# Three moves in a fused decoder kernel: the gates' sums behind the first adapter round, GpSimd's sums released by the third norm's low parts, and the rank-4 product in wide instructions

## The reference

```python
x = x + attn(layernorm(x))            # scores q k^T, scaled; banded by sigmoid(score); softmax; values; projection
x = x + xattn(layernorm(x), ctx, ctx) # 8 heads; gates i, f from [q, k, v]; csum = cumsum(log_sigmoid(f)) along tokens
                                      # D = exp(csum_i - csum_j + i_j - max); (q k^T * D / tau) v / normalizer; head norm
x = x + ffn(layernorm(x))
```

```python
even, odd = lt[:, ::2, :], lt[:, 1::2, :]
m1 = (even[:, :4, :, None] * odd[:, :4, None, :]).reshape(Bx, Hx, Dx)
m2 = (even[:, 4:, :, None] * odd[:, 4:, None, :]).reshape(Bx, Dx, Hx)
h = x @ W1.T + scale * einsum('bsd,bhd->bsh', x, m1) + b1;  h = gelu(h)
out = h @ W2.T + scale * einsum('bsh,boh->bso', h, m2) + b2
```

## Time and profile before

| | |
|---|---|
| median of 3 runs | 2023.12 us (2022.67 to 2023.55) |
| profiled execution | 2027.77 us, span 2026.0 us |
| TensorE, matmul busy | 1940.2 us (96%) |
| VectorE busy | 1522.6 us (75%) |
| ScalarE busy | 1125.0 us (56%) |
| GpSimd busy | 314.9 us (16%) |
| granted TensorE clock, mean | 0.986 of full speed |

### The profile page before, as it was taken

One profiled execution on the slowest core, in us unless ns is written; L12 is line 12 of the kernel. 1 busy time (PEld: TensorE's weight loads), 2 busy tenths in 40 slices (PEclk: granted clock), 3 DMA queues, 4 the chain that ended last, 5 costly groups with the idle time before them and its releaser, 6 DMA issues.

```text
span 2026.0 us, 47964 instructions
## 1 busy us (share of the span) xinstructions
PE 1940.2 (96%) x16404; PEld 1464.9 (72%) x16404; DVE 1522.6 (75%) x4318; ACT 1125.0 (56%) x2504; POOL 314.9 (16%) x257
## 2 busy tenths in 40 slices
PE   5789999999999999999999999999999999999988
PEld 4467777777777777777777777777777777777766
DVE  6577787778787778777778778777878777877742
ACT  2455566655556655556655556665555665555551
POOL 1111011111011111111111101111101111111110
PEclk9699999999999999999999999999999999999999
DMA  3000001110001111010110000011000111100000
GB/s 103 22 23 14 30 22 32 32 32 31 12 22 32 32 32 32 11 32 22 32 32 32 17 27 22 32 32 32 32 12 22 32 32 32 32 11 33 13 13 22
DMA packets 65583, 56.43 MB, mean 28 GB/s; under 512 B 13185, under 2 KB 65026, under 8 KB 65554
## 3 DMA queue, kind: packets, MB, share of 16 engines
q1 hardware_dynamic: 65554, 56.05, 8.9%
HBM read 37.15 MB, written 16.78 MB: 27 GB/s over the span
## 4 chain that ended last, share of the span: by engine, by line
PE 93%; DVE 4%; ACT 2%; issue 0%; DMA 0%; SPq 0%; DVEq 0%; ACTq 0%
PE UA L1290 16%; PE UB L1290 5%; PE TB L1232 5%; PE UB L1232 5%; PE UA L1232 5%; PE PV L1232 4%; PE UA L1240 3%; PE TA L1257 3%; PE TB L1372 3%; PE GT L1302 3%; PE TA L1372 3%; PE TA L1197 3%; PE TA L1101 3%; PE TB L1101 3%; PE QQ L1086 2%; PE UA L1310 2%
## 5 line engine op out<-in xcount | busy, mean ns | idle before, releaser
L1290 PE MATMUL UA<-W2f,hs_all 128*128 128x256 f32 x1536 | 349.1, 380 | 2.9 <-DVE ot L943 2.2
L1290 PEld LDWEIGHTS UA<-W2f,hs_all 128*128 128x128 f32 x1536 | 286.5, 190 | 62.3 <-issue 13.9
L957 DVE TENSOR_TENSOR C<-qT,QKs 128x512 f32<-128x512 f32 x256 | 169.3, 690 | 172.3 <-ACT qT L668 153.4
L550 POOL TENSOR_TENSOR Ng<-HT,gnw_b 128x256 f32<-128x256 f32 x128 | 94.9, 741 | 820.4 <-ACT HT L681 820.4
L531 POOL TENSOR_TENSOR xg<-x,gnb_b 128x1024 f32<-128x1024 f32 x32 | 75.9, 2372 | 811.1 <-DVE csum L893 811.1
L1290 PE MATMUL UB<-W2f,hs_all 128*128 128x256 f32 x512 | 115.8, 379 | 0.0
L659 ACT ACTIVATE hs_all<-UA,b1c 128x512 f32<-128x512 f32 x64 | 44.0, 687 | 109.6 <-PE TB L1240 109.6
L1290 PEld LDWEIGHTS UB<-W2f,hs_all 128*128 128x128 f32 x512 | 94.9, 190 | 11.7
L649 ACT ACTIVATE QKs<-TA 128x512 f32<-128x512 f32 x64 | 38.4, 600 | 108.9 <-PE DD L1257 108.9
L1257 PEld LDWEIGHTS TA<-xn2T,ctxT 32*128 32x128 f32 x512 | 63.2, 190 | 30.1 <-issue 27.7
L898 DVE TENSOR_SCALAR band_a<-sc 128x512 f32<-128x512 f32 x32 | 76.7, 2397 | 10.0 <-ACT sc L633 10.0
(11 more groups left out here) (311 smaller groups left out, 5532.3 us busy)
## 6 DMA issues: line engine op xcount, KB each, us to landing
xin<-x SPq DMA_DIRECT2D x32, 512.0 KB, 3.5
ctxn<-ctx SPq DMA_DIRECT2D x32, 512.0 KB, 3.8
out<-ot SPq DMA_DIRECT2D x32, 512.0 KB, 3.0
Ev<-xn SPq DMA_DIRECT2D x512, 1.0 KB
hs_all<-L_ffn_W SPq DMA_DIRECT2D x4, 512.0 KB, 8.7
T<-tok SPq DMA_DIRECT2D x128, 2.0 KB
moving<-parts SPq DMA_DIRECT2D x96, 8.0 KB, 1.9
QKs<-L_attn_W_qkv SPq DMA_DIRECT2D x1, 768.0 KB
```

Source lines behind the costliest of these rows:

```text
L550: pool.tensor_tensor(Ng[:, b, :].rearrange("p (k n) -> p k n", k=2), HT[:, b % 2, :, 0:P], gnw_b[:, :].rearrange("p (k n) -> p k n", k=2), ...
L957: dve.tensor_tensor(C[:, b % 2, 4 * hf:4 * hf + 4, :].rearrange("p h i -> p (h i)"), dx[hf], QKs[:, b, 4 * hf:4 * hf + 4, :].rearrange("p ...
L1290: ins = pe.matmul(OB[b][:, 0:D], hs_all[:, k, b * S:(b + 1) * S], W2f[:, k, :], start=(i == 0), stop=(i == KH - 1))
```

## The change

It has four parts.

1. `sums()` moves on TensorE from behind `up(2)` to behind `up_adapter(0)`.
2. GpSimd's first instruction of a step waits for `xn3l_ok` (both low parts written) instead of `csum_ok`. Its other waits stay.
3. `low_rank()` gives each product all 512 columns: 8 products (16 instructions in the profile) instead of 32 (64). `Zo` is packed to 32 columns, four used of each eight, a sequence to each eight. So each product also multiplies the tokens of one sequence with the rank-4 rows of the others.
4. `gT_copy` sets those foreign entries to zero: it adds `bias_row` and multiplies by `own_g`, which holds `scale` where partition and sequence belong together, 1 in the bias row and 0 elsewhere. `own_g` is made at setup from `sel_g`: on GpSimd one memset and one select more, on VectorE one reduction and one small instruction more.

```diff
--- before.py
+++ after.py
@@ -170,6 +170,8 @@
         W1h = sb("W1h", [P, KD, HID], F32R)
         W1l = sb("W1l", [P, KD, HID], F32R)
         W2f = sb("W2f", [P, KH, D])
+        own_g = sb("own_g", [P, G])
+        sel_g = sb("sel_g", [P, G, CB * R])
         bias_row = sb("bias_row", [P, 1])
         pick = sb("pick", [96, 32], BF16)
         ident_h = sb("ident_h", [P, P], BF16)
@@ -238,7 +240,7 @@
 
         Z = sb("Z", [P, KD, G, 32])
         tok = sb("tok", [P, S])
-        Zo = sb("Zo", [P, KD, 40 * G])
+        Zo = sb("Zo", [P, KD, 32])
         E = sb("E", [P, 2, P])
         T = sb("T", [P, N])
         Ev = sb("Ev", [P, D])
@@ -512,10 +514,14 @@
             pool.memset(vc[:, :, HD - 1::HD], 1.0)
             pool.memset(ones[:, :], 1.0)
             pool.memset(lntau[:, :], LN_TAU)
-            pool.memset(bias_row[:, :], 0.0).then_inc(s_idz, 1)
+            pool.memset(bias_row[:, :], 0.0)
+            pool.memset(sel_g[:, :, :], 0.0).then_inc(s_idz, 1)
             pool.wait_ge(s_idz, 3)
             pool.affine_select(out=bias_row[:, :], in_=bias_row[:, :], compare_op=ALU.not_equal, fill=1.0,
                                base=-BIAS_ROW, pattern=[[-1, 1]], channel_multiplier=1)
+            v = sel_g[:, :, :].rearrange("p b (c r) -> p b c r", c=CB)
+            pool.affine_select(out=v, in_=v, compare_op=ALU.not_equal, fill=1.0, base=0,
+                               pattern=[[-8, G], [-32, CB], [-1, R]], channel_multiplier=1)
             for t in (WgT, Z, Zo, E, T, Ev, em):
                 pool.memset(t[tuple([slice(None)] * len(t.shape))], 0.0)
             pool.memset(gbias[:, :], 0.0).then_inc(s_zero, 1)
@@ -527,7 +533,7 @@
                     pool.wait_ge(x2_ok.h, x2_ok.at(it, 0))
                     pool.wait_ge(xn_ok[2].h, xn_ok[2].at(it, 0))
                     pool.wait_ge(xf_ok.h, xf_ok.at(it, 1))
-                    pool.wait_ge(csum_ok.h, csum_ok.at(it, 1))
+                    pool.wait_ge(xn3l_ok.h, xn3l_ok.at(it, 2))
                     pool.tensor_tensor(xg[:, :, :], x2[:, :, :], gnb_b[:, :].unsqueeze(1).broadcast_to([P, G, D]),
                                        ALU.add).then_inc(xg_ok.h, 1)
                 if SELF.on(it):
@@ -836,6 +842,8 @@
             n += 1
             dve.wait_ge(s_set_pe, n)
             dve.wait_ge(s_zero, 1)
+            done(dve.tensor_reduce(own_g[:, :], sel_g[:, :, :], AX_X, ALU.add))
+            done(dve.tensor_scalar(own_g[:, :], own_g[:, :], sc_b[:, 0:1], bias_row[:, 0:1], ALU.mult, ALU.add))
             dve.wait_ge(s_gbias, 16 * (2 * G + 1))
             done(dve.tensor_copy(WgT[:, :, 0:16], PV[:, 0:64].rearrange("p (k n) -> p k n", k=4)))
             done(dve.tensor_copy(pick[32:64, :], pick[0:32, :]))
@@ -946,8 +954,10 @@
 
                     dve.wait_ge(gT_mm.h, gT_mm.at(it, 1))
                     dve.wait_ge(adapt_mm.h, adapt_mm.at(it, 0))
-                    dve.tensor_scalar(gT[:, :], GT[:, :], sc_b[:, 0:1], bias_row[:, 0:1], ALU.mult, ALU.add)\
-                       .then_inc(gT_ok.h, 1)
+                    dve.scalar_tensor_tensor(gT[:, :].rearrange("p (b s) -> p b s", b=G),
+                                             GT[:, :].rearrange("p (b s) -> p b s", b=G), bias_row[:, 0:1],
+                                             own_g[:, :].unsqueeze(2).broadcast_to([P, G, S]),
+                                             ALU.add, ALU.mult).then_inc(gT_ok.h, 1)
 
                 def weigh_qk(b, hf):
                     k = 2 * b + hf
@@ -1265,10 +1275,10 @@
                         up(i)
                     if i == 0 and cross:
                         gates()
-                    elif i == 2 and cross:
-                        sums()
                 if ffn:
                     up_adapter(0)
+                if cross:
+                    sums()
                 for i in range(4, KH):
                     if ffn:
                         up(i)
@@ -1295,12 +1305,10 @@
                     pe.wait_ge(zo_ok.h, zo_ok.at(it, 1))
                     pe.wait_ge(QKs_ok.h, QKs_ok.at(it, 8))
                     pe.wait_ge(h_ok.h, h_ok.at(it, KH))
-                    for b in range(G):
-                        tok_b = slice(b * S, (b + 1) * S)
-                        for k in range(KD):
-                            for c in range(CB):
-                                ins = pe.matmul(GT[32 * c:32 * c + 32, tok_b], Zo[:, k, 32 * b:32 * b + 32],
-                                                hs_all[:, KD * c + k, tok_b], start=(k == 0), stop=(k == 1))
+                    for k in range(KD):
+                        for c in range(CB):
+                            ins = pe.matmul(GT[32 * c:32 * c + 32, :], Zo[:, k, :], hs_all[:, KD * c + k, :],
+                                            start=(k == 0), stop=(k == 1))
                     ins.then_inc(gT_mm.h, 1)
 
                 def adapt(b):
@@ -1449,7 +1457,7 @@
 LOADS = 2 * KD + CB + 3
 V_WT = 7 + 2 + 1
 V_BIAS = V_WT + 2 + 2 + 2 + 4
-SETUP_V = V_BIAS + 1 + 2 + 1 + 8 + 1
+SETUP_V = V_BIAS + 2 + 1 + 2 + 1 + 8 + 1
 
 
 def kernel(**inputs):
```

## The result

The changed kernel takes 1991.62 us (median of 4 runs, 1991.01 to 1994.47) against 2022.89 for the kernel before on the same chip: a ratio of 0.9848, 95% interval 0.9831 to 0.9865. The profiled execution took 1994.47 us, 33.3 less than before's 2027.77; the forecast's sum was 33.2. The medians lie 31.3 apart, and single executions of one kernel differ by up to 7 us (2020.78 to 2027.97 in 15 of the kernel before), so the agreement of the two sums to 0.1 us is closer than either can be told.

A forecast was written before the change was run, and what follows sets the result against it. TensorE was taken to bound the kernel, with a 0.76 us hole per step. Gains of 30.1 (sums), 1.9 (product) and 1.5 (step 1), less 0.3 (setup), make 33.2 us: 2023.1 to 1990 us, range 1985 to 2005.

The forecast's parts named there:

- the forecast's sum: All terms over the whole kernel: 30.1 + 1.9 + 1.5 - 0.3 = 33.2 us saved.
- The bound: TensorE, busy for 96% of the span, bounds the kernel; each 60.12 us step has one hole of 0.76 us.
- Sums moved, 0.97 us a step: TensorE's sums fill the Gelu hole (0.77 us) and TB's projection shortens (0.20 us); 30.1 us over 31 steps.
- GpSimd's release, worth nothing: GpSimd's three sums start 3.0 us earlier; `acs` margin before QK grows from 0.07 to 0.5 us, no time counted.
- The wide product, -0.06 us a step: The rank-4 product on TensorE takes 1.82 us instead of 1.88, gaining 1.9 us over 32 steps.
- my estimate of 2.24 us: The wide product's time by the skill's packing speedup of 3.07: 0.36 us more than now, total 13 us higher.
- Once: One-time terms: setup on VectorE loses 0.3 us; step 1's wait for `acs` shrinks by 1.5 us.
- The scan as what TensorE waits for: Rival: VectorE's `csum` misses its place between GpSimd's instructions and delays TensorE's sums; 2024.7 us, no change, chance 0.07.
- The wide product in series: Rival: the product's column groups run one after another, up to 6.9 us a step; 2152 us, slower, chance 0.06.
- The sign would turn: The change was to become slower once the wide product takes over 2.89 us.

The follow-up runs named there:

- the other filling: Kernel before with sums ahead of the first adapter round, VectorE's `acs` copy ahead of its second band instruction, first QK products in the hole: 1978.04 us, ratio 0.9775.

## Why the prediction was right, point by point

**The bound.** TensorE's order with one hole per step: right. The hole was all the idle time there was; after, the windows count TensorE as busy in all of the 59.16 us. That busy time can still shrink by order alone is shown by the other filling, 58.66.

**Sums moved, 0.97 us a step.** Right in size and in both parts, given GpSimd's release: the step without the wide product is 0.98 us shorter (60.12 to 59.14); 0.22 of it shows alone with the sums ahead of the adapters. The projection behind the hole gave nothing back (1.65 against 1.67).

**GpSimd's release, worth nothing.** This step failed, though the total did not. I compared the end of `acs` with the start of the QK products, and left out the 0.26 us that pass between them. The earlier trace rows could have told it only indirectly; the chain of step 1 has it in both kernels, as 0.24 and 0.25 us of issue between `acs` and the first QK product. So the margin with the sums moved alone was negative by 0.2 us, TensorE waits 0.2 to 0.3 us a step, and the release gives it back. The total held because I summed up the kernel with both parts, where 0.65 us lie between the two (1025.54 to 1026.19), 0.4 of them beyond the hand-over. How `lsig`, `csum` and the bands would meet GpSimd came out within 0.3 us: `csum` ended 0.8 us ahead of the sums where I had 0.9.

**The wide product, -0.06 us a step.** The mechanism (four groups side by side) was right; the term was mis-sized: 1.85, not 1.82, and 0.05 us a step came back through the place of tensors in SBUF, which I didn't think of. Net 0.01 to 0.02 us a step lost, so of the 1.9 us of the sum nothing came. The Trainium skill ("TensorE: Matmul & The Clock Gate", Measured speedup vs the span model) has its 3.07 for four row groups; my estimate of 2.24 us by this figure isn't borne out by the 1.85 of four column groups here.

**Once.** Setup: `own_g`'s small instruction takes 2.17 us behind GpSimd, and `pick` 0.16 behind it: it is the wait that moved. `moving` starts 1.25 us later than before, 0.81 of which was there ahead of `own_g`: a loss of 0.44 (0.3 foreseen); the reduction took 0.22, not 0.41. Step 1 begins 1.3 us late and its decay products start at 92.22 in place of 92.23: a gain of 1.3 (1.5 foreseen), which only makes up for the late start.

**The sum.** That 33.2 met 33.3 is luck beyond the steps. 31 steps of 0.96 us make 29.8 (30.1 foreseen). The product gave nothing (1.9 foreseen), and up to step 1's decay products the two kernels are level (1.2 foreseen). Some 3.5 us stand in no term: they come from stretches at the start and the end in which TensorE has the lower clock, and which are shorter in the profiled execution of the changed kernel. The first window below ends with step 2's first projection, the second with the gates' products of step 32; two windows of the kernel before, then the same two of the changed kernel:

```profile
127.60:132.30 4.70, 4.68 (x34) 3.72 (x38) 3.06 (x13) 2.14 (x3) 0.00 (x0) 0.64 0.03 5
1930.99:1937.84 6.85, 6.85 (x63) 5.15 (x63) 1.44 (x4) 2.25 (x3) 0.00 (x0) 0.55 0.25 80
```

```profile
126.80:129.90 3.10, 3.10 (x34) 2.35 (x38) 3.04 (x13) 1.83 (x3) 0.00 (x0) 1.00 0.02 6
1899.86:1905.51 5.65, 5.65 (x63) 4.21 (x63) 1.43 (x4) 2.22 (x3) 1.68 (x1) 0.70 0.28 94
```

They give 1.6 and 1.2 us, and 0.8 comes the same way behind step 1's decay products (granted clock 0.50 before and 0.66 after from 96 to 100 us, 0.91 and 1.00 from 100 to 104). Whether the change brings this or the one execution does isn't shown. The first stretch is as short in both other kernels that have GpSimd's release and one set of sums, but not in that with the sums twice.

**The rivals.** The scan as what TensorE waits for did not come. `lsig` stood ready 0.36 us before `xg` ended (1019.77 against 1020.13) and took the place ahead of `x`; only if it had missed that place would `csum` have missed the next. What the scan costs when TensorE asks earlier is in the run with the release alone, 62 us. The wide product in series was nowhere. (The sign would turn at 2.86 us, not 2.89: 31.3 us over 32 steps.)

## What to carry to other kernels

A hole in the bounding engine's queue is filled by moving into it work that nobody on the way to the hole's end needs; price it as the smaller of the two, and look whether the place it leaves was costing something as well (a change between full and 32-wide products on TensorE here, 0.2 us on each side). When such a move brings a consumer forward, compare its start with its producer's end plus the hand-over that the trace has for this very pair, not with the end alone. Two engines that exclude each other should collide where the bounding engine isn't waiting, and a release that is a loss of 62 us alone can be a gain of 9 with the move that it belongs to.

## What the runs showed of the hardware

- Where TensorE had waited about 2 us in a step, the granted clock stood at its lower level, 1.2 GHz, behind the wait in some steps: 0.53 of full speed over the 3.2 us from 1060.20, in which one projection took 2.70 instead of 1.58 us; 11 of 27 steps there, 7 of 28 with GpSimd's release alone. In the kernel before, with waits of 0.76 us, all steps that the chain shows take 60.12 us, at 1.00 where I read it.
- 272 bytes of unused SBUF per partition cost 0.05 us a step, 512 bytes none (one execution each): the same up projection takes 1.41 or 1.38 us by where the tensors declared later lie, its inputs `xn3h` and `xn3l` among them.
- TensorE pays about 0.2 us both on entering and on leaving a group of 32-wide f32 products between the projections: the QK products take 1.10 us behind a projection and 0.90 behind the adapters, and the projection behind the sums 1.60 instead of 1.40. Behind f32 transposes of full width the projection pays nothing (1.38).
- VectorE's scan with two SBUF inputs took 2.64 us instead of 0.42, having started 0.04 us after a GpSimd instruction of 2.40 us.
- From a VectorE instruction's end to the TensorE product that waits for it pass 0.04 us at the sums and 0.24 to 0.26 us at the QK products.
